# A transformer block with attention on one core: denominators summed once per iteration, and the feed-forward's first block prepared in other buffers

## The reference

```python
c6 = silu(c) @ Wc + bc                     # shift, scale, gate, twice
xm = ln(x) * (1 + sc_msa) + sh_msa
q, k, v = xm @ Wq + bq, xm @ Wk + bk, xm @ Wv + bv
w = softmax((q / 32) @ k^T);  y = w @ v
x = x + g_msa * (y @ Wo + bo)
xm2 = ln(x) * (1 + sc_mlp) + sh_mlp
x = x + g_mlp * (gelu(xm2 @ W1 + b1) @ W2 + b2)
```

## Time and profile before

| | us |
|---|---|
| median of 3 runs (2742.05 to 2742.95) | 2742.39 |
| profiled execution, its own time | 2740.38 |
| its span, first to last instruction | 2738.6 |
| PE busy in the span | 2699.0 |
| POOL busy in the span | 1868.1 |
| first scores of attention | 345.29 |
| first scores of iteration 31 | 1860.87 |
| feed-forward begins | 1933.80 |

### The profile page before, as it was taken

The page is one execution under the profiler, slowest core; times in us unless marked ns, Lnnn a source line. Parts: engine busy times, 40 slices in busy tenths (PEclk is TensorE's granted clock), DMA queues, the critical chain, the costliest instruction groups (busy, mean ns, idle before and its releaser), DMA issues. The chain is left out here.

```text
span 2738.6 us, 37946 instructions
## 1 busy us (share of the span) xinstructions
PE 2699.0 (99%) x13737; PEld 1780.1 (65%) x13737; DVE 1996.4 (73%) x3322; ACT 1345.6 (49%) x2538; POOL 1868.1 (68%) x1080
## 2 busy tenths in 40 slices
PE   7999999999999999999999999999999999999998
PEld 5777755555555555555555555554688888888887
DVE  6557688888888888888888888875575765765754
ACT  2322267666766667666666766676221221221211
POOL 1000088989989998999989989895555555455553
PEclk9999999999999999999999999999999999999999
DMA  6555468788888879878788887874410110110000
GB/s 246 204 188 169 153 131 174 169 184 174 184 179 177 187 163 189 187 164 187 174 185 182 173 186 168 197 153 117 147 35 16 46 36 11 47 47 0 31 16 16
DMA packets 143754, 369.22 MB, mean 135 GB/s; under 512 B 23572, under 2 KB 40528, under 8 KB 119760
## 3 DMA queue, kind: packets, MB, share of 16 engines
q0 software_dynamic: 26784, 195.05, 35.6%
q1 hardware_dynamic: 96000, 155.26, 18.9%
q10 hardware_dynamic: 20784, 16.49, 2.0%
HBM read 111.97 MB, written 58.97 MB: 62 GB/s over the span
## 5 line engine op out<-in xcount | busy, mean ns | idle before, releaser
L1073 DVE TENSOR_REDUCE part_max<-shared_bank 128x1 f32<-128x512 f32 x1972 | 1207.6, 681 | 273.9 <-PE shared_bank L1193 273.9
L1048 ACT ACTIVATE probs<-s_bank 128x512 f32<-128x512 f32 x2048 | 1036.7, 629 | 292.0 <-PE s_bank L1209 288.8
L1220 PE MATMUL y_bank<-probs,vs 128*32 128x512 f32 x4096 | 497.3, 603 | 0.0
L895 POOL TENSOR_TENSOR first_sum<-probs 128x1024 f32<-128x1024 f32 x124 | 339.3, 2736 | 81.7 <-ACT probs L1048 79.5
L1636 ACT ACTIVATE h<-shared_bank,vecs 128x512 f32<-128x512 f32 x128 | 87.9, 687 | 563.0 <-PE shared_bank L1660 558.2
L1209 PE MATMUL s_bank<-late_parts 97*128 97x512 f32 x848 | 349.1, 413 | 0.7 <-ACT probs L1048 0.7
L895 POOL TENSOR_TENSOR half_sum<-probs 128x1024 f32<-128x1024 f32 x124 | 336.1, 2722 | 15.6 <-ACT probs L1048 15.5
L1193 PE MATMUL shared_bank<-late_parts 96*128 96x512 f32 x848 | 337.0, 398 | 0.9
L906 POOL TENSOR_TENSOR wo<-probs 128x1024 f32<-128x1024 f32 x124 | 333.4, 3033 | 1.1 <-ACT probs L1048 1.1
L906 POOL TENSOR_TENSOR second_sum<-probs 128x1024 f32<-128x1024 f32 x128 | 317.6, 2619 | 16.0 <-ACT probs L1048 10.2
L1446 POOL TENSOR_TENSOR late_parts<-w_raw,late_parts 128x512 fp32r<-128x512 f32 x96 | 128.9, 1343 | 226.6 <-DVE late_parts L1523 226.6
(11 more groups left out here) (209 smaller groups left out, 4553.9 us busy)
## 6 DMA issues: line engine op xcount, KB each, us to landing
half_sum<-second_sum POOLq DMA_DIRECT2D x62, 1024.0 KB, 13.5
first_sum<-wo POOLq DMA_DIRECT2D x62, 1024.0 KB, 9.8
half_sum<-first_sum POOLq DMA_DIRECT2D x62, 1024.0 KB, 7.5
q_parts<-qk_out SPq DMA_DIRECT2D x32, 512.0 KB, 3.1
k_parts<-qk_out SPq DMA_DIRECT2D x32, 512.0 KB, 3.5
late_parts<-q_parts SPq DMA_DIRECT2D x63, 256.0 KB, 11.6
late_parts<-k_parts SPq DMA_DIRECT2D x60, 256.0 KB, 11.7
late_plain<-in_x SPq DMA_DIRECT2D x12, 1024.0 KB, 7.1
```

The costliest lines, as they stand in the source:

```text
L895: pool.tensor_tensor(first_home(c)[:, hs, :], probs[:, 4 * c % RING, hs, :], probs[:, (4 * c + 1) % RING, hs, :], ALU.add).then_inc(first_ ...
L1048: act.activation(probs[:, tile % RING, h, :], s_bank[(HPG * tile + h) % 3][:, :], ACT.Exp).then_inc(p_done, 1)
L1073: v.tensor_reduce(part_max[:, i % 2, hs, c:c + 1], m_bank[ring.bank["max", i, n]][:, :], AX.X, ALU.max).then_inc(m_taken, 1)
L1220: last = pe.matmul(y_bank[h * DH:(h + 1) * DH, :], vs[:, t, h * DH:(h + 1) * DH], probs[:, tile % RING, h, :], start=(t == 0), stop=(t == ...
```

## The change

1. **Start.** `w_lo[:, 0]` (POOL) and `w_lo[:, 1]` (DVE) are made in four instructions of 128 x 512 each, and PE waits for the latter piece by piece in its second product group.
2. **Memory.** The gates go to DRAM at the end of `project` (2 MB) and are loaded again: two rows for the first block at the start of attention, six at the start of the feed-forward. The space gives a fourth `half_sum` and a third `y_buf`.
3. **One denominator group an iteration.** A further accumulating transfer, `fold_whole`, adds an iteration's two half sums, issued by POOL in the next iteration's third quad. `sums(u)` comes once for each iteration, at t = 1 two iterations later, and ahead of `times_v`. There is one copy, one small transfer and no addition on DVE. Everything behind it is one iteration later. `take_sum` stands at the start of t = 2, and `take_y` at the start of t = 3.
4. **First block's preparation.** The low parts are written over their sources, in other spaces; ACT rounds y in iteration 29 and biases it in 30; DVE makes all low parts by one instruction of 128 x 2048 right after iteration 30's maxima; x is loaded in iteration 30. The 48 products of `first_out` come one behind each score, from s = 48 of iteration 30 to s = 31 of iteration 31, with the products that need low parts of y later.
5. **Last quads.** POOL adds the third and the fourth tile onto DVE's first pair (`last_adds`, four half operations a quad in place of two), and PE sums one buffer a quad. `modulate_first` goes from ACT to DVE.

```diff
-    return ((b - 9) // 4,) if b >= 9 and b % 4 == 1 else ()
+    return ((b - 16) // 8,) if b >= 16 and b % 8 == 0 else ()
...
-            WO_LO_AT = (LAST_QUAD - 6, LAST_QUAD - 5, LAST_QUAD - 4, LAST_QUAD - 3)
+            WO_LO_AT = (LAST_QUAD - 10, LAST_QUAD - 8, LAST_QUAD - 6, LAST_QUAD - 4)
...
+            def last_adds(c):
+                home, q = first_home(c), c - LAST_QUAD
+                for n, hs in enumerate(PAIR):
+                    pool.wait_ge(last_first_ready, 2 * q + n + 1)
+                    pool.wait_ge(p_done, HPG * (4 * c + 2) + hs.stop)
+                    pool.tensor_tensor(home[:, hs, :], home[:, hs, :], probs[:, (4 * c + 2) % RING, hs, :], ALU.add).then_inc(last_third_ready, 1)
+                for n, hs in enumerate(PAIR):
+                    pool.wait_ge(last_third_ready, 2 * q + n + 1)
+                    pool.wait_ge(p_done, HPG * (4 * c + 3) + hs.stop)
+                    pool.tensor_tensor(home[:, hs, :], home[:, hs, :], probs[:, (4 * c + 3) % RING, hs, :], ALU.add).then_inc(second_ready, 1)
...
+            def fold_whole(i):
+                pool.wait_ge(half_folded, 16 * (2 * i + 2))
+                accumulate(half_sum[2 * i % HALVES][:, :, :], half_sum[(2 * i + 1) % HALVES][:, :, :]).then_inc(whole_folded, 16)
...
-                if c % QPI == QPI - 2 and c // QPI >= 2:
-                    normalise(c // QPI - 2)
+                if c % QPI == QPI - 2 and 1 <= c // QPI < LAST:
+                    fold_whole(c // QPI - 1)
+                if c % QPI == QPI - 2 and c // QPI >= 3:
+                    normalise(c // QPI - 3)
...
-                    if t == 2 and i:
+                    if t == 3 and i:
                         take_y(i - 1)
-                    if tile >= 20 and tile % 8 == 4 and (tile - 20) // 8 < LAST_HALF:
-                        take_sum((tile - 20) // 8)
+                    if t == 2 and i >= 2:
+                        take_sum(i - 2)
...
-            OUT_FROM = 6
+            OUT_FROM = N_SC * (N_IT - 2) + 48
...
                     if t % 2 == 1:
                         b = (NKT * i + t) // 2
+                        if b % 8 == 0:
+                            for u in due_sums(b):
+                                sums(u)
                         if b:
                             times_v(2 * b - 2)
                             times_v(2 * b - 1)
```

More of the change, by code:

```diff
@@ L40 @@
 RING = 5
[L41 to L43 removed]
+LAST = N_IT - 1
+HALVES = 4
 EARLY_LEAD, LEAD, BEFORE = 12, 20, 3
@@ L371, in _ @@
             pool.wait_ge(w_hi_ready, 1)
-            pool.tensor_tensor(w_lo[:, 0, :, :], w_raw[0], w_hi[:, 0, :, :].bitcast(F32), ALU.subtract).then_inc(w_split[0], 1)
+            for t in range(KT):
+                last = pool.tensor_tensor(w_lo[:, 0, t, :], w_raw[0][:, t, :], w_hi[:, 0, t, :].bitcast(F32), ALU.subtract)
+            last.then_inc(w_split[0], 1)
             for k in range(1, NBLK):
@@ L739, in last_banks @@
     def last_banks(self):
-        held = [self.bank["sum", LAST_HALF + n] for n in (-2, -1, 0)]
+        held = [self.bank["sum", LAST + n] for n in (-2, -1, 0)]
         unused, = set(range(self.BANKS)) - set(held)
@@ L767, in attend @@
         probs = sb("probs", [P, RING, HPG, TOK])
-        half_sum = [sb(f"half_sum{n}", [P, HPG, TOK]) for n in range(3)]
+        half_sum = [sb(f"half_sum{n}", [P, HPG, TOK]) for n in range(HALVES)]
         first_sum = [sb(f"first_sum{n}", [P, HPG, TOK]) for n in range(2)]
@@ new lines, in sums @@
+                if u == LAST:
+                    pe.wait_ge(feed.wo_taken, 1 + OUT_BANKS.index(3) + 1)
+                if u < LAST - 1:
+                    pe.wait_ge(whole_folded, 16 * (u + 1))
+                    for h in range(HPG):
+                        last = add_up(u, h, half_sum[2 * u % HALVES][:, h, :], True, True)
+                elif u == LAST - 1:
+                    pe.wait_ge(half_folded, 16 * (2 * u + 2))
+                    for h in range(HPG):
+                        add_up(u, h, half_sum[2 * u % HALVES][:, h, :], True, False)
+                        last = add_up(u, h, half_sum[(2 * u + 1) % HALVES][:, h, :], False, True)
+                else:
+                    c = LAST_QUAD + u - LAST
@@ L1268, in first_transposes @@
+                if last:
+                    ins.then_inc(feed.wo_done, 1)
             def first_transposes(t):
@@ L1360, in gate @@
         def gate(b, which):
-            return sh.gates[:, bass.ds(b, 1), which, :].rearrange("p a n -> p (a n)")
+            return feed.first_gates[:, which, :] if 4 * b + which < 2 else gates[:, 4 * b + which - 2, :]
         @block.sync
@@ L1385, in _ @@
             load_w2(1)
+            sp.dma_start(gates[:, :, :], sh.gate_rows[:, 2:4 * B, :]).then_inc(gates_in, 16)
+            sp.wait_ge(late.y_normed, N_IT - 2)
             sp.wait_ge(late.inv_stored, 16 * (N_IT - 1))
```

295 lines of the change are left out of this document (163 added, 132 removed).

## The result

The changed kernel takes **2734.2 us** (median of 9 runs, 2732.8 to 2737.6) against 2742.1 us for the kernel before (9 runs beside it). The ratio is 0.9976, 95% interval 0.9967 to 0.9986: a gain of 7.8 us (by the interval 3.8 to 9.0) where 23.8 were forecast. The profiled execution has a span of 2734.4 us, where the one before had 2738.6.

The account below looks back on a forecast made before the run. Attention was taken to be paced by PE's own list. Terms -26.4 + 10.2 + 2 - 2.6 - 7.0 - 0.5 + 0.5 = -23.8 us, from 2742.4, gave 2718.6 us; range 2699 to 2739.

Parts of the forecast that it names:

- iteration 31: Last attention iteration: shorter blocks give -12.1 us, 5.1 given back for POOL's added work; -7.0 us, bounds -12.1 and +1.
- DVE's one instruction for the low parts: End of iteration 30: if it is late, only s = 0 of iteration 31 waits for it; no cost priced.
- rival 3: Last quads: POOL and DVE exclude each other, iteration 31 gets 4 us longer; -12.8 us in all, 2730 us, chance 0.20.
- eight more half operations of POOL: Iteration 31: 2.5 us each, 20 us, set against POOL's idle 19.7 + 5.3 us; 5.1 us given back.
- The groups: Denominator groups on PE, 70 before and 36 after: 31 of those removed save 0.85 us each, -26.4 us.
- The stall of y's copy: `take_y` in mid-block delays an exponential, so PE loses 0.33 us in each of 31 iterations: +10.2 us, 0 to 15.5.
- The new fold: Extra POOL issue and transfer each iteration, some folds landing later: +2 us for all iterations, 0 to 31.
- End of iteration 30: Last two blocks, with an output product behind each score, become ordinary: 2 x 5.80 for 14.24 us, -2.6 us.
- Start: Before attention: waits around the `w_lo` splits shrink, but only what DVE's chain gains stays; -0.5 us, -2 to 0.
- Feed-forward: Start of the feed-forward: SP also waits for an inverse ahead of the weight load; +0.5 us, 0 to 2.

Follow-up runs that it names:

- e1: Changed kernel plus one wait: POOL's y normalisation in iteration 30's third quad waits until DVE has written the low parts of the first block's y; 2733.2 us.
- e7: Changed kernel with both POOL's wait for the low parts of y and the last four quads added up as in the kernel before; 2725.9 us.
- e5: Changed kernel with the last four quads added up as in the kernel before: POOL's second buffer, two PE groups a quad; 2728.3 us.
- e4: Changed kernel without the new DMA addition of an iteration's two halves; PE sums both halves, two groups an iteration; 2753.4 us.
- e6: Changed kernel with ACT's copy of y moved to t = 2, behind the copy of the sums; 2732.3 us.
- e3: Changed kernel with ACT's copy of y moved to t = 2, ahead of the copy of the sums; 2736.8 us.
- e13: e8 plus a POOL wait for DVE's first half-quad sums ahead of its biases, and the half's fold issued behind the first pair's second part; 2716.9 us.
- e11: e8 without the new DMA addition of an iteration's two halves; PE sums both halves; 2735.8 us.
- e8: Changed kernel with the edits of e1, e5 and e6 together, the new fold kept; 2723.4 us.
- e2: Changed kernel with the low parts of y written by four DVE instructions of 128x512 in place of one of 128x2048; 2740.7 us.

## Why the prediction missed

**The step that failed** is iteration 31, at -7.0 us; it measured +9.8. That the time still lies in the wide range of 2699 to 2739 is owed to the range and not to the working. Two sentences carried the step.

- "If DVE's one instruction for the low parts is late, only s = 0 of iteration 31 waits for it", priced at nothing. The wait was 9.07 us. I had the 6.63 us row of two blocked operations and named the exclusion, but gave it a price only in rival 3, for the last quads. While POOL had its next instruction ready DVE was not served at all, and POOL had 19.4 us of work in a row. What undoing this is worth was shown by e1 and e7: 3.5 to 4.6 us in the profiles, 1.0 to 2.4 by the medians.
- The eight more half operations of POOL, for which I gave back 5.1 us by adding them up against POOL's idle time. They cost 7.9 to 9.0 us (e5, e7; 5.9 to 7.3 by the medians), net of the 3.5 us that four more groups on PE cost in these kernels. From the changed kernel to e5, 5.7 us lie behind block 6 and 2.9 in block 5. The first came through DVE, whose splits took 2.6 to 2.8 us in place of 0.4 and 0.7, with PE waiting 5.6 us for them; the second through POOL's order, where the root for the norm stood behind four half additions and DVE waited 4.6 us for it. Idle time of POOL in a stretch was the wrong measure, as it was DVE that needed it. The start was too early as well: I let POOL's biases begin 4.9 us into the iteration, though 3.0 + 2.6 gives 5.6, and they began at 8.6.

The second is rival 3, with chance 0.20 and "4 us longer"; its mechanism was right, its size was less than half of what came. The first was in no rival. Without both (e7), iteration 31 has 70.2 us, 2.7 under the kernel before, and its blocks show where the rest of the forecast went. "Forecast" is the prediction's working before it gave back 5.1 us:

| us | before | forecast | changed | e7 |
|---|---|---|---|---|
| blocks 0 to 3 | 30.0 | 24.4 | 35.2 | 24.6 |
| block 4 | 5.4 | 5.4 | 5.4 | 5.4 |
| block 5 | 8.9 | 8.9 | 12.7 | 17.2 |
| block 6 | 9.3 | 7.5 | 7.2 | 8.0 |
| block 7, to the feed-forward | 19.3 | 14.6 | 22.2 | 14.9 |

So outside block 5 the forecast of PE's list came out within 0.5 us a row, in part by luck, since e7 has four groups (3.5 us) more on PE than it counted. What stands against it in e7 is block 5, 8.3 us: the first block's norm hangs on a root in POOL's order, and there the root comes 11.3 us into the block (1.0 us ahead of it before, 2.5 into it in the changed kernel). In e7 it stands behind the wait for the last fold; the prediction had no term for this. The Trainium skill (SBUF — State Buffer, "Who interferes with whom") has the lock and says, of VectorE's modes that use both ports, that whoever issues first holds it for the whole instruction. e1 agrees with the lock (21.60 to 3.60 us). But by that reading DVE, waiting since 1833.70, would have had its turn behind the POOL operation that was running; the trace shows it passed over by all that followed.

**The groups** (-26.4): 0.87 us each by e4, and 0.83 from the kernel before to e6 (48.76 to 47.93); forecast 0.85. Right.

**The stall of y's copy** (+10.2, 0.33 each): 0.36. Right, and for the reason given; e6 removes it and e3 shows that the order of the two copies decides.

**The new fold** (+2, 0 to 31): in the changed kernel 2.4 us of late iterations. Right in size, but e6 to e13 show what the number hid: POOL and its transfers had little left. With the stall gone an iteration took 48.2 to 48.4 us on average where PE alone needs 47.9. The 11 us stall of y's copy was also their cover. The fold brings 20.6 us with the stall (e4 to e7) and 10.0 without it (e11 to e8; 16 if e6's faster iterations stand for e8's). What makes the iterations late is open: POOL is busy 45.2 of 48.4 us, the DMA engines 0.96 of the time, and no run tells a full DMA queue from POOL's instructions or from the order of its waits. e13 moved one wait and had less late time (5.4 for 11.4), which the scatter and the low clock could give too; the kernels meant to remove the others brought a new wait each.

**End of iteration 30** (-2.6): two blocks of 5.79 and 5.84 us for 14.24, right. **Start** (-0.5): +0.2; the wait moved on along DVE's chain, and was mis-sized only. **Feed-forward** (+0.5): +1.1. Its first block is 0.5 us shorter (101.33 for 101.82), the ones behind it take 101.65 us in place of 101.47 from block to block, PE busy throughout; what makes the same products longer is open, no run tried it.

## What to carry to other kernels

Before adding GpSimd work next to a VectorE operation with two SBUF inputs, don't sum busy times: ask whether GpSimd has a gap at that point, and if the VectorE operation is on the path, make GpSimd wait for it. The longest stall that a profile shows is not what its removal is worth; the same resource may bind again a few instructions later, so remove the competitor, not the instance. A stall on the pacing engine is slack for all others: before costing its removal, look at the runner-up's margin: here POOL and its transfers gave 48.2 to 48.4 us an iteration on average when PE stood at 48.3.

## What the runs showed of the hardware

A VectorE tensor-tensor of 128x2048 takes 2.29 us with POOL quiet (e7) and took 21.60 us under a row of POOL operations; four of 128x512, 0.69 us each alone (e7), took 26.06 us (e2). A wait of one engine for the other, which is no computation at all, gave it its turn: 3.60 us in e1 and 2.29 in e7, where POOL stood idle for 1.4 and 3.4 us. The max reductions, which read PSUM, ran at a mean of 0.68 us all the while beside the same POOL load.
